# Side sort: low and slot one-hots built from 32-bit integers instead of from ScalarE's 16-bit copies

## The reference

```python
edge_index = jnp.stack([src, dst])                       # 200,000 edges, graph "gnn"
x = x + _L0_gnn_ref(xn, edge_index, ...) + _L0_mix_ref(xn[None], ...)[0]
x = x + _L0_ffn_ref(_layernorm(x)[None], ..., L0_ffn_edge_index)[0]   # 131,072 edges, graph "gat"
# gt_layer: q, k, v of each edge's end nodes, att = exp(clip(q . k)), segment sums over the edges' rows
```

## Time and profile before

| what | value |
|---|---|
| median of 3 runs | 7432.77 us (7426.59 to 7434.32) |
| the profiled execution, its own time | 7436.28 us |
| its span, first to last instruction | 7434.6 us |
| granted TensorE clock, mean | 0.760 of full |
| busy: PE / DVE / ACT / POOL | 5178.4 / 5381.4 / 2567.8 / 5053.4 us |
| costliest group | L695 on POOL, 3336 gathers of att1 and att2, 3278.6 us |

### The profile page before, as it was taken

The page is one execution under the profiler, slowest core; times in us unless marked ns, Lnnn a source line. Parts: engine busy times, 40 slices in busy tenths (PEclk is TensorE's granted clock), DMA queues, the critical chain, the costliest instruction groups (busy, mean ns, idle before and its releaser), DMA issues. The chain is left out here.

```text
span 7434.6 us, 108730 instructions
## 1 busy us (share of the span) xinstructions
PE 5178.4 (70%) x27327; PEld 4108.7 (55%) x27327; DVE 5381.4 (72%) x15227; ACT 2567.8 (35%) x8277; POOL 5053.4 (68%) x5420
## 2 busy tenths in 40 slices
PE   5985676767777776466666666666679999998440
PEld 3654455556666665256656555555546666665330
DVE  8983676667777776467777777776767777777997
ACT  0002444443344433344444444444322222222330
POOL 1430677777777776577777777777267777776991
PEclk7558788887878777777777888888668888887555
DMA  1013544444444443444444444444323323232437
GB/s 27 4 26 92 138 138 137 139 130 122 124 121 124 124 124 110 112 132 131 131 131 131 131 131 131 131 131 129 106 52 63 60 59 63 59 63 60 121 92 185
DMA packets 510444, 783.73 MB, mean 105 GB/s; under 512 B 121690, under 2 KB 370617, under 8 KB 509837
## 3 DMA queue, kind: packets, MB, share of 16 engines
q0 software_dynamic: 202656, 454.22, 23.2%
q1 hardware_dynamic: 299233, 311.35, 15.5%
q10 hardware_dynamic: 7948, 11.21, 0.6%
HBM read 705.00 MB, written 71.36 MB: 104 GB/s over the span
## 5 line engine op out<-in xcount | busy, mean ns | idle before, releaser
L695 POOL DMA_INDIRECT att_kv_e<-kv,gnn_idx x3336 | 3278.6, 983 | 1238.2 <-issue 984.7
L772 PE MATMUL att_ps_sum<-att_vals,att_hot 128*125 128x136 f32 x6672 | 1290.7, 350 | 1358.1 <-DVE att_vals L826 1356.8
L772 PEld LDWEIGHTS att_ps_sum<-att_vals,att_hot 128*125 128x125 f32 x6672 | 1095.9, 238 | 1588.7 <-DVE att_vals L826 1572.4
L695 POOL DMA_INDIRECT max_rows<-rows,gat_idx x1128 | 1065.6, 945 | 469.5 <-issue 337.4
L807 DVE TENSOR_TENSOR att_prod<-att_ps_q,att_kv_e 128x512 f32<-128x512 f32 x834 | 575.9, 691 | 990.0 <-issue 401.9
L759 PE MATMUL att_ps_q<-qs,att_hot_t 125*128 x6672 | 1182.1, 336 | 104.8 <-DVE att_hot_t L814 104.8
L759 PEld LDWEIGHTS att_ps_q<-qs,att_hot_t 125*128 125x128 f32 x6672 | 1127.8, 254 | 106.1 <-issue 106.1
L790 ACT ACTIVATE att_hot<-node_no,gnn_loc 128x125 f32<-128x125 f32 x3336 | 1044.4, 384 | 22.8 <-PEq L86 22.8
L783 ACT ACTIVATE att_ps_dve<-att_clipped 128x32 f32<-128x32 f32 x834 | 167.7, 201 | 2442.0 <-DVE att_clipped L834 2441.3
L2399 DVE CUSTOM_DVE_ANT_0 max_junk<-max_far,max_ps_b 125x256 bf16<-125x256 bf16 x2256 | 793.3, 416 | 260.2 <-PE max_ps_b L2363 258.7
L842 DVE TENSOR_TENSOR acc<-acc,att_ps_sum 125x136 f32 x1668 | 485.6, 291 | 125.2 <-DVE acc L842 8.2
(11 more groups left out here) (450 smaller groups left out, 7501.2 us busy)
## 6 DMA issues: line engine op xcount, KB each, us to landing
att_local<-gnn_loc_rows SPq DMA_DIRECT2D x834, 128.0 KB
att_kv_e<-kv,gnn_idx POOLq DMA_INDIRECT x3336
max_local<-gat_loc_rows SPq DMA_DIRECT2D x282, 128.0 KB
gs_local<-gat_loc_rows SPq DMA_DIRECT2D x141, 256.0 KB, 3.2
outs<-ex_y SPq DMA_DIRECT2D x25, 896.0 KB
max_rows<-rows,gat_idx POOLq DMA_INDIRECT x1128
X<-in_x SPq DMA_DIRECT2D x10, 1120.0 KB
ans_late<-outs SPq DMA_DIRECT2D x11, 896.0 KB
```

Source lines behind the costliest of these rows:

```text
L695: pool.indirect_dma_start(rows(j, e), None, source, bass.IndirectOffsetOnAxis(ap=g.idx[:, t:t + 1], axis=0))\
L772: ins = pe.matmul(ps_sum[j % 2][0:NODE_TILE, p * 256:p * 256 + SUMS], hot[:, j, PAIR * p + e, :], vals[:, j % 2, PAIR * p + e, :], start=e ...
```

## The change

The two 16-bit copies and their tiles `low` and `slot` go, with the semaphores `low16` and `slot16` and ScalarE's whole part in the side sort. L1366 and L1372 keep their first operand and their output (16-bit) and take as second operand the 32-bit tiles `low_i` and `slot_i`, broadcast as before. They wait for VectorE's own semaphores `low` and `slot`. L1354, which overwrites `low_i`, waits for the products of the block before (`spread`, four per block) in place of `slot16`.

```diff
-        self.low, self.slot = sb(p, [BLOCK], F16), sb(p, [BLOCK], F16)
...
             dve.wait_ge(m["reduced"], ROUNDS * (k + 1))
-            wait(dve, m["slot16"], k)
+            wait(dve, m["spread"], 4 * k)
             dve.tensor_scalar(self.low_i, self.place_i, 4, LANES - 1, ALU.arith_shift_right, ALU.bitwise_and)\
                 .then_inc(m["low"], 1)
...
-                dve.wait_ge(m["low16"], k + 1)
+                dve.wait_ge(m["low"], k + 1)
                 wait(dve, m["permuted"], k)
                 rows = slice(half * LANES // 2, (half + 1) * LANES // 2)
                 dve.tensor_tensor(self.hot_low[:, rows], self.s.low_no[0:p, rows],
-                                  self.low.unsqueeze(1).broadcast_to([p, LANES // 2, BLOCK]), ALU.is_equal)\
+                                  self.low_i.unsqueeze(1).broadcast_to([p, LANES // 2, BLOCK]), ALU.is_equal)\
                     .then_inc(m["spread"], 1)
...
-            dve.wait_ge(m["slot16"], k + 1)
+            dve.wait_ge(m["slot"], k + 1)
             step(dve.tensor_tensor(self.hot_slot, self.s.low_no[0:p, OWN // LANES:OWN // LANES + SLOTS_F],
-                                   self.slot.unsqueeze(1).broadcast_to([p, SLOTS_F, BLOCK]), ALU.is_equal))
+                                   self.slot_i.unsqueeze(1).broadcast_to([p, SLOTS_F, BLOCK]), ALU.is_equal))
...
-    def scalar(self, act, n):
-        m = self.m
-        k = self.block_at(n, 8)
-        if k is not None:
-            act.wait_ge(m["low"], k + 1)
-            wait(act, m["spread"], 4 * k)
-            act.copy(self.low, self.low_i).then_inc(m["low16"], 1)
-            act.wait_ge(m["slot"], k + 1)
-            act.copy(self.slot, self.slot_i).then_inc(m["slot16"], 1)
```

More of the change, by code:

```diff
@@ L1090, in __init__ @@
                                           "dests", "dest_ready", "owners", "tile_ready", "tiles_out", "cleared",
-                                          "base_in", "hots", "ranked", "reduced", "low", "slot", "low16", "slot16",
-                                          "spread", "permuted", "records"])
+                                          "base_in", "hots", "ranked", "reduced", "low", "slot", "spread", "permuted", "records"])
         self.last = LOOP + LOOP_PACE * (blocks - 1) + 20
@@ L1508, in scalar @@
         self.keys.scalar(act, n)
-        self.sort.scalar(act, n)
 class Mix:
```

## The result

The changed kernel takes 7533.5 us (median of 4 runs, 7522.1 to 7538.6) against 7431.8 us for the kernel before (4 runs, one more than in the table of the time before, 7426.6 to 7434.3): a ratio of 1.0136, 95% interval 1.0118 to 1.0153. The profiled execution took 7532.7 us, with a span of 7531.0 us. The changed kernel has two lines fewer ahead of the loop: L1366 is L1364 after the change, L1372 is L1370, L1378 is L1376.

A forecast was written before the change was run, and what follows sets the result against it. POOL's gathers were taken to bound the side sort's loop: longer holds of 71.8 + 25.4 = 97.2 us, added to the profiled 7436.3, give 7533.5, less 3.5 for the median: 7530.0 us, 8-in-10 range 7500 to 7556.

The forecast's parts named there:

- What bounds the loop: Side sort's loop: POOL is full, 948 gathers each costing its duration plus a fixed 0.30 us gap; VectorE follows.
- The duration of the mixed form: L1366 and L1372 run at the 32-bit pace, 2816 and 2151 ns, growing by 1.33 and 1.00 us.
- ScalarE's copies and the waits at nothing: Side sort: dropping 11.6 us of ScalarE copies gains nothing; the changed waits are met on arrival and cost nothing.
- The hold: Loop gathers starting in L1366 or L1372 wait until it ends: 71.8 plus 25.4 us more in POOL.
- With the same start: Each of 54 L1366 begins where it did against its gather, which is held 1.33 us more: 71.8 us.
- the 1.25 us rhythm: POOL in the loop: gathers start every 0.946 + 0.30 = 1.25 us, so every longer L1366 holds one.
- the port given back: Rival, loop gathers: slower 32-bit L1366 and L1372 release POOL, 51.3 us of stretches go, 7381 us; chance 0.05.
- nothing moves: Rival, L1366 and L1372: mixed form as fast as now, or its longer part hidden; 7433 us; chance 0.07.
- VectorE falls behind: Rival, loop: POOL starts to wait for `weighted`, at most 98.8 us on top, 7629 us; chance 0.03.
- 10 and 11: Profile rows: scan L1216 stretched a gather by 2.23 us, product L1628 by 0.25, as 32-bit two-SBUF-operand evidence.
- the rule of the remaining time less 0.14: A held gather is stretched by what is left of the VectorE instruction at its start, less 0.14 us.
- holds a little: L814, one tensor operand in SBUF, was said to hold gathers only 5.6 us over 235 rounds, untouched by the change.

The follow-up runs named there:

- e4: The change, but with the 32-bit tiles `low_i` and `slot_i` in the PSUM bank of the exponentials; 7382.9 us, ratio 0.9928 to the kernel before.
- e7: On top of e4, the block's digits copied to PSUM as 32-bit floats, from where L1378 multiplies by them; 7364.8 us, ratio 0.9902.
- e3: The kernel before with ScalarE's copies `low` and `slot` kept but made as 32-bit floats; 7528.1 us, ratio 1.0130.
- e2: The kernel before plus an unused 32-bit reduction of one SBUF operand behind each L1366 and each L1372; 7442.2 us, ratio 1.0010.
- e1: The kernel before with only L1366 comparing with the 32-bit integers; slot one-hot and its 16-bit copy stay; 7506.5 us, ratio 1.0097.
- e6: The kernel before with each 16-bit L1366 cut into four instructions of 640 elements; 7411.7 us, ratio 0.9963.
- e8: The change with each 32-bit low one-hot (L1366 before) cut into four instructions of 640 elements; 7461.2 us, ratio 1.0036.

## Why the prediction was right

*What bounds the loop*: right. POOL's gaps stayed at 0.305 us in the changed kernel and in e4 and e7, and the loop was as long as its gathers in each.

*The duration of the mixed form*: right, 2824 and 2153 ns against 2816 and 2151. It was the one cost with ends far apart, and e3 shows the choice was good for the stated reason, the width.

*ScalarE's copies and the waits at nothing*: right; e3 keeps them and takes the time of the change.

*The hold*: right in mechanism. By the timelines of both kernels, each stretch put to the VectorE instruction that ran 0.14 us after the gather's start, the terms are:

| us held | before | after | added | predicted |
|---|---|---|---|---|
| L1366 | 37.8 | 112.4 | 74.6 | 71.8 |
| L1372 | 13.5 | 42.8 | 29.3 | 25.4 |
| L1378 | 23.3 | 18.2 | -5.1 | 0 |
| L1325 and L814 | 10.3 | 6.0 | -4.3 | 0 |

The first two were each a little low. "With the same start" was the weak step: the starts moved. After the change 35 of the 54 L1364 met a gather at one of two places, 14 of them 0.1 to 0.2 us after their own start and 21 about 0.6 us (on average at 0.62 us, after 0.66 before), and 16 of the 27 L1370 met it 0.14 us after theirs, where the hold is 1.89 us. The last two rows fell, so that the sum of the four rows, 94.5 us, came out within 3 us of the 97.2. That two errors met is luck; that they are small is, as argued from the pace of the gathers, the 1.25 us rhythm, which bounds every shift.

*The time*: forecast 97.2 us more; the median moved by 101.7 us, the profiled execution by 96.4, and the four runs of the change lie within 16.6 us.

*The rivals*: the port given back is excluded by the maximum of 3.56 us. What it got right is the size of the prize, 51.3 us, which e4 collected (7434.3 - 7382.9 = 51.4 us) by taking the second operand away rather than slowing the instruction. That nothing moves is excluded by the result, and that VectorE falls behind by e2 and by POOL's gaps, still 0.305 us in the changed kernel.

*Two readings were weaker than they were put.* Only two rows, 10 and 11, were given for the "three" that show 32-bit work holding a gather, and the scan of the earlier trace rows doesn't fit the rule of the remaining time less 0.14: it had 2.08 us left and the stretch was 2.23, where the same scan in the changed kernel had 2.09 us left and stretched its gather by 1.88. And "holds a little" for L814, with one tensor operand in SBUF, was read from the sum. In the kernel before, 71 gathers started in an L814 with over 0.25 us of it left, and 66 of them were stretched by more than 0.1 us. Its sum is small because L814 is short, 0.48 us. Neither changed the forecast.

The rule of the Trainium skill on two SBUF inputs (SBUF — State Buffer, section "SBUF: two separate sides") agrees with these runs where VectorE starts first: two inputs in SBUF hold a gather (e1, e3, the change), one input in SBUF and one in PSUM doesn't (e4, e7), and the lock is one instruction long (e6, e8). The section also says that the lock goes to whichever of the two starts first, and that the other waits; that VectorE waits for a gather which started first is not seen here. In the kernel before, 43 of the 54 L1366 began while a gather was running; they took 1486 ns in the median, and so did the other 11.

## What to carry to other kernels

When GpSimd generates gathers and is the bound, price a VectorE instruction by where its operands lie, not by its own time: one with two tensors in SBUF costs GpSimd up to its whole length, one with one of its two tensors in PSUM cost nothing here, even at twice the length. One tensor operand alone is no safe sign: reductions held no gather, but `tensor_scalar` and casts from SBUF to SBUF did (L814, and L1264, a 54x1000 cast with 0.52 us left that stretched a gather by 0.40). Look for it in the maximum of the gathers' duration, not in any wait; the profile counts a held engine as busy. Where no operand can be moved, shorter instructions hold less.

## What was not expected

VectorE's work and the gathers fall into step with each other, so that a hold taken away at one place can come back at another: L1378, untouched in all of them, held 23.3 us in the kernel before, 18.2 after the change, 28.1 in e2 and 36.0 in e8. Why the starts gather at certain places of the rhythm was not looked into; that VectorE's rounds begin with the landing of a gather is a likely reason, and only argued.

VectorE took the 125x2560 comparison in 2815 ns with the 32-bit operand in PSUM and 2821 ns with it in SBUF: at this width, PSUM costs VectorE nothing.
